# Means of the last six tiles by two DMAs through a DRAM row instead of TensorE transpositions

## What is computed

```python
xn = (x - mean(x)) / sqrt(var(x) + 1e-5)                # 2048 tokens x 512
q  = xn @ Wq.T + bq                                     # only every fourth head: 8 heads of 128
s  = elu(q) + 1
a  = s / (sum(s * z, per head) + 1e-6)
attn = repeat(a @ M, 4 heads) @ Wo.T                    # = a @ P, P = M @ (sum of Wo over the 4)
out  = x + attn + (xn @ (w * w_scale) + b)
```

## Time and profile before

| | us |
|---|---|
| median of 3 runs | 243.72 (243.65 to 243.77) |
| the profiled execution | 243.56 |
| its span, first to last instruction | 241.7 |
| PE busy | 234.1 (97%) |
| DVE busy | 178.0 (74%) |
| ACT busy | 119.6 (49%) |
| POOL busy | 108.4 (45%) |

### The profile page before, as it was taken

One profiled execution on the slowest core, in us unless ns is written; L12 is line 12 of the kernel. 1 busy time (PEld: TensorE's weight loads), 2 busy tenths in 40 slices (PEclk: granted clock), 3 DMA queues, 4 the chain that ended last, 5 costly groups with the idle time before them and its releaser, 6 DMA issues.

```text
span 241.7 us, 3385 instructions
## 1 busy us (share of the span) xinstructions
PE 234.1 (97%) x1030; PEld 186.7 (77%) x1030; DVE 178.0 (74%) x266; ACT 119.6 (49%) x276; POOL 108.4 (45%) x108
## 2 busy tenths in 40 slices
PE   8699999998999999999999999999999999999995
PEld 2488788885776788888888888888888888788885
DVE  2889695897998669887687694958666778995631
ACT  2654626628648923655463526455463747341110
POOL 1058734756271815553434326263403629657500
PEclk9999999999999999999999999999999999999999
DMA  7999999999370211424252515221212223244441
GB/s 225 405 417 411 383 242 225 216 217 217 94 252 5 53 51 52 127 54 126 53 168 53 161 50 169 52 91 42 88 52 73 56 75 108 76 136 136 133 174 44
DMA packets 21985, 34.83 MB, mean 144 GB/s; under 512 B 5200, under 2 KB 13136, under 8 KB 20816
## 3 DMA queue, kind: packets, MB, share of 16 engines
q1 hardware_dynamic: 19344, 26.63, 33.4%
q0 software_dynamic: 1376, 6.82, 13.4%
q10 hardware_dynamic: 1248, 1.18, 1.8%
HBM read 22.02 MB, written 4.19 MB: 108 GB/s over the span
## 4 chain that ended last, share of the span: by engine, by line
PE 33%; issue 31%; POOL 18%; DVE 8%; SPq 4%; DMA 2%; ACT 2%; ACTq 1%; POOLq 0%; DVEq 0%
POOL e_and_sz L313 9%; POOL xT L288 5%; PE attn_ps L793 4%; PE attn_ps L794 4%; PE attn_ps L795 4%; SPq L219 4%; POOL x L321 3%; PE q_ps L793 3%; PE q_ps L795 3%; PE q_ps L794 3%; DVE aT_lo L654 2%; PE dense_ps L793 2%; PE dense_ps L795 2%; PE dense_ps L794 2%; DMA xT<-in_xT 2%
## 5 line engine op out<-in xcount | busy, mean ns | idle before, releaser
L313 POOL TENSOR_TENSOR e_and_sz<-s,z_b 128x512 f32<-128x512 f32 x32 | 42.0, 1340 | 40.3 <-DVE den L633 40.2
L441 ACT ACTIVATE s<-s,rden 128x128 f32<-128x128 f32 x128 | 39.2, 389 | 40.5 <-DVE rden L637 40.5
L793 PE MATMUL attn_ps<-P_hi,aT_hi 128*128 128x512 f32 (+1 forms) x128 | 49.8, 389 | 0.5 <-DVE aT_lo L654 0.5
L795 PE MATMUL attn_ps<-P_hi,aT_lo 128*128 128x512 f32 (+1 forms) x128 | 49.1, 383 | 0.0
L794 PE MATMUL attn_ps<-P_lo,aT_hi 128*128 128x512 f32 (+1 forms) x128 | 49.0, 383 | 0.0
L793 PE MATMUL q_ps<-WqT_hi,xT_hi 128*128 128x512 f32 x104 | 42.1, 405 | 0.3 <-DVE s L628 0.3
L795 PE MATMUL q_ps<-WqT_hi,xT_lo 128*128 128x512 f32 x104 | 40.6, 390 | 0.0
L794 PE MATMUL q_ps<-WqT_lo,xT_hi 128*128 128x512 f32 x104 | 40.5, 389 | 0.0
L288 POOL TENSOR_TENSOR xT<-xT,mean_b 128x512 f32<-128x512 f32 x13 | 18.3, 1408 | 37.8 <-ACT mean_b L390 31.2
L621 DVE SCALAR_TENSOR_TENSOR q_ps<-q_ps,rstd,bq_b 128x512 f32<-128x512 f32 x28 | 21.0, 753 | 19.3 <-PE q_ps L795 19.3
L793 PEld LDWEIGHTS attn_ps<-P_hi,aT_hi 128*128 128x128 f32 x128 | 24.1, 188 | 6.2 <-issue 0.9
(11 more groups left out here) (82 smaller groups left out, 365.3 us busy)
## 6 DMA issues: line engine op xcount, KB each, us to landing
x<-in_WoT POOLq DMA_DIRECT2D x6, 1024.0 KB, 10.6
x<-in_x SPq DMA_DIRECT2D x16, 256.0 KB, 3.9
xT<-in_xT SPq DMA_DIRECT2D x16, 256.0 KB, 4.1
aT<-s SPq DMA_DIRECT2D x124, 32.0 KB, 1.9
out<-x SPq DMA_DIRECT2D x15, 256.0 KB, 2.3
MT<-s SPq DMA_DIRECT2D x96, 32.0 KB, 1.9
x<-in_WoT SPq DMA_DIRECT2D x2, 1024.0 KB, 14.0
s<-in_WqT SPq DMA_DIRECT2D x2, 512.0 KB, 7.1
```

The costliest lines, as they stand in the source:

```text
L313: nc.gpsimd.tensor_tensor(sz_eps[:, :, h * D // 2:(h + 1) * D // 2].rearrange("p g (j c) -> p j g c", j=2), by_quarter(sbuf_s[:, t % SRING ...
L441: last = nc.scalar.activation(a_g, a_g, ACT.Copy, scale=rden[:, t % 2, g:g + 1])
L793: nc.tensor.matmul(out, x_hi, w_hi, start=start, stop=False)
L795: return nc.tensor.matmul(out, x_lo, w_hi, start=False, stop=stop)
```

## The change

Tiles 0 to 9 keep their way. For tiles 10 to 15 (FIRST_BY_DMA is LEAD + 3 = 10), in steps 8 to 13:

- PE doesn't do `spread_mean(t + 2)`, and ACT doesn't do `copy_mean(t + 2)`.
- SP, after the loads of its step and ahead of `spread_blocks(t - 4)`, waits for bn_aggr of tile t + 2 and sends the column meanvar[:, t + 2, 0:1] (128 partitions, 4 bytes each) to row t + 2 of a new DRAM tensor, mean_rows: `line_up_mean`.
- ACT, at the place where copy_mean stood, waits until that row has landed (and for the buffer of mean_b, as copy_mean did) and issues a transfer that reads the row of 512 bytes into all 128 partitions of mean_b: `spread_mean_row`.
- POOL's `center` waits for the landing of that transfer instead of copy_mean.

```diff
--- before.py
+++ after.py
@@ -34,6 +34,7 @@
     XRING = 4
     HRING = 4
     BEHIND = 3
+    FIRST_BY_DMA = LEAD + 3
     assert P == D and HID == 512 and HALF == 512 and R == 4 and T == 16 and G == 8 and K == 4
 
     with ExitStack() as ctx:
@@ -65,6 +66,7 @@
         aT_hi = sb("aT_hi", [P, 2, G, P], F32R)
         aT_lo = sb("aT_lo", [P, 2, G, P], F32R)
         mean_b = sb("mean_b", [P, 2, P])
+        mean_rows = nc.dram_tensor("mean_rows", (T, P), F32)
         ident = sb("ident", [P, P])
         e_and_sz = sb("e_and_sz", [P, E + G * (D + 1)])
         neg_half = sb("neg_half", [P, 1])
@@ -116,6 +118,8 @@
         rstd_ready = sem("rstd_ready")
         mean_filled = sem("mean_filled")
         mean_copied = sem("mean_copied")
+        mean_row_in = [sem(f"mean_row_in{i}") for i in range(2)]
+        mean_b_in = [sem(f"mean_b_in{i}") for i in range(2)]
         xc_by_dve = sem("xc_by_dve")
         xc_by_pool = sem("xc_by_pool")
         xT_hi_ready = sem("xT_hi_ready")
@@ -219,6 +223,10 @@
                         sp.dma_start(aT_place(t)[j * 32:(j + 1) * 32, i, :],
                                      sbuf_s[i * 32:(i + 1) * 32, t % SRING, j * E // 4:(j + 1) * E // 4]
                                      ).then_inc(aT_in[in_MT(t)], 16)
+
+            def line_up_mean(t):
+                sp.wait_ge(meanvar_ready, t + 1)
+                sp.dma_start(mean_rows[t].unsqueeze(1), meanvar[:, t, 0:1]).then_inc(mean_row_in[t % 2], 16)
 
             def store(t):
                 sp.wait_ge(attn_added, t + 1)
@@ -261,6 +269,8 @@
                     sp.wait_ge(P_filled, t + 4 - FIRST_LENT + 1)
                     load_x(t + 4)
                     load_xT(t + 4)
+                if FIRST_BY_DMA <= t + 2 < T:
+                    line_up_mean(t + 2)
                 spread_blocks(t - BEHIND - 1)
                 if t - LEAD >= 1:
                     store(t - LEAD - 1)
@@ -283,7 +293,10 @@
                                         ).then_inc(rstd_ready, 1)
 
             def center(t):
-                pool.wait_ge(mean_copied, t - 2)
+                if t < FIRST_BY_DMA:
+                    pool.wait_ge(mean_copied, t - 2)
+                else:
+                    pool.wait_ge(mean_b_in[t % 2], 16 * ((t - FIRST_BY_DMA) // 2 + 1))
                 pool.wait_ge(xT_in[t], 16)
                 nc.gpsimd.tensor_tensor(xT[:, t % XRING, :, :], xT[:, t % XRING, :, :],
                                         mean_b[:, t % 2, :].unsqueeze(1).to_broadcast([P, K, P]), ALU.subtract
@@ -389,6 +402,11 @@
                     act.wait_ge(xc_by_pool, t - 4)
                 nc.scalar.activation(mean_b[:, t % 2, :], mean_ps[:, 0:P], ACT.Copy
                                      ).then_inc(mean_copied, 1)
+
+            def spread_mean_row(t):
+                act.wait_ge(mean_row_in[t % 2], 16 * ((t - FIRST_BY_DMA) // 2 + 1))
+                act.wait_ge(xc_by_pool, t - 4)
+                act.dma_start(mean_b[:, t % 2, :], mean_rows[t].unsqueeze(0).to_broadcast([P, P])).then_inc(mean_b_in[t % 2], 16)
 
             def copy_first_xT_hi(j):
                 act.wait_ge(xc_by_dve, j + 1)
@@ -526,8 +544,10 @@
                 if t == LEAD:
                     copy_P_hi(7)
                 copy_aT_hi(t - LEAD + 1)
-                if t + 2 < T:
+                if t + 2 < FIRST_BY_DMA:
                     copy_mean(t + 2)
+                elif t + 2 < T:
+                    spread_mean_row(t + 2)
                 for u in denominators_of_step(t):
                     if u < T - 2:
                         make_a(u)
```

## The result

The changed kernel takes 267.08 us (median of 6 runs, 265.94 to 268.94) against 243.69 us before: 1.0968 times as long (95% interval 1.0924 to 1.1012), 23.4 us slower where 1.3 were forecast. The profiled execution took 266.57 us, its span is 264.8.

A forecast was written before the change was run, and what follows sets the result against it. TensorE, busy 97% of the span, was taken as the bound; 0.66 us saved on transpositions and a 2.0 us stall at product_q(10, 0) gave +1.3 us on 243.72, so 245.0 us, range 243.9 to 246.7.

The forecast's parts named there:

- What bounds the kernel, and SyncE's backlog: Steps 8 to 13: TensorE's own work sets the pace; backlogged SyncE sends tile 10's row only at 110.24, mean ready at 96.38.
- the forecast's 119.3: Tile 10: predicted start of product_q(10, 0), wanted by TensorE at 117.31, so a stall of 2.0 us.
- 5.95: Tile 10: predicted us from the row's landing, through ScalarE's and VectorE's queued work, to TensorE's start of product_q(10, 0).
- I take 3.1 ... The bounds are 112.5 and 114.1: First transfer, tile 10: the row sent at 110.24 lands after 3.1 us, at 113.35, between those bounds.
- Rival (d): The two transfers in series bound tile 10: first 4.2 to 5 us, second 3; time 246.3 to 247.5; chance 12%.
- One stall, then, and not six: Tiles 10 to 15: TensorE stalls 2.0 us at product_q(10, 0) only; later tiles' rows come in time.
- The slack of 0.85 us at tile 11: product_q(11, 0): xT_lo(11) reaches TensorE at 132.05, wanted at 132.9, so the wait is hidden by 0.85 us.
- The second transfer: ScalarE's broadcast of the row into all partitions: lands 1.9 to 2.6 us after it is issued.
- It just hides behind make_a and exp.: Tile 10: the broadcast and centering let copy_xT_hi start by 3.4 to 4.2 us after landing; ScalarE's queue gets there at 4.24.
- The transpositions: TensorE, tiles 10 to 15: six removed at 0.11 us each save 0.66 us.
- SyncE's six added issues at 0: SyncE, steps 8 to 13: six issues of 0.53 us make 3.2 us, nearly all absorbed, so costed at 0.
- the spare 1.9 us: SyncE ahead of spread_blocks(10): about 1.9 us idle waiting for VectorE, expected to take up the added issues.

The follow-up runs named there:

- e8: The changed kernel with SyncE sending each tile's column of means one step sooner, still as adjacent 4-byte pieces: 244.12 us, ratio 1.0001.
- e2: The changed kernel with the first transfer as one 512-byte piece, a row of the identity, so wrong means are taken off: 245.03 us.
- e5: The kernel before, with one unused extra transfer of a different form on ScalarE's queue in each of steps 8 to 13: 243.88 us.
- e12: The changed kernel with the row's pieces 512 bytes apart in DRAM and the second transfer reading input b (wrong means), second run: 245.65 us.
- e10: The changed kernel with ScalarE's wait for the row and the second transfer moved behind make_a: 264.02 us.
- e4: The changed kernel without the first transfer; ScalarE issues the second at once from input b (wrong means): 242.58 us, ratio 0.9952.
- e1: The kernel before, plus the change's first transfer, for which nobody waits; means still go through TensorE: 243.59 us, ratio 0.9999.
- e7: The changed kernel with VectorE turning the means into four 128-byte pieces and ScalarE sending both transfers, the row behind exp_of(t, 0): 242.78 us, ratio 0.9955.
- e6: The changed kernel with both transfers on ScalarE, adjacent 4-byte pieces kept, its wait for the row behind make_a: 248.82 us, ratio 1.0185.
- e11: The changed kernel with VectorE turning the means so SyncE sends four 128-byte pieces at the change's own place: 247.16 us, ratio 1.0124.

## Why the prediction was wrong

**What bounds the kernel, and SyncE's backlog: right.** The row left at 111.57 (forecast 110.24; the load of x ahead of it took 1.28 us to issue in place of 0.58), ScalarE stood still from 101.4, GpSimd, copy_xT_hi, split_xT_lo and product_q(10, 0) followed in that order. e8 shows that the place is the other half of the cause: with the same slow row a step sooner there is no stall at any product_q. product_q(10, 0) started 8.0 us later than the forecast's 119.3: 5.3 by the landing, 1.3 by the row's later start and 1.4 by the way from the landing to TensorE (7.3 us in place of 5.95).

**The step that failed is the landing of the row, "I take 3.1 ... The bounds are 112.5 and 114.1".** It landed at 120.0, after 8.4 us. The bound from above, 3.8, was "the slowest of the transfers here", and all of those move pieces of 1 KB or more; I wrote that no row shows a write of 128 pieces and bounded it as if size didn't matter. Rival (d) had the right mechanism, the first transfer slow, and stopped at 5 us. e2 shows that no other term was off by much: with a landing of at most 2.3 us the time is 245.03, the forecast's 245.0. The sentence of the Trainium skill on writes to HBM ("DMA: Bandwidth & Descriptors", section on the anatomy of one DMA), weighed in (d), pointed the right way but not at the cause: e5 and e12 write the same pieces to the same memory in 2.6 and 2.8 us.

**"One stall, then, and not six" failed with it.** The slack of 0.85 us at tile 11 rested on a landing of 2.6 to 3.0. With 8 to 10 us the queues close a loop that the prediction left out, since it never asked what SyncE would come to wait for. The row of tile 10 holds ScalarE; so split_aT_lo(3) ends at 130.63; spread_blocks(5) waits for that and starts at 130.70; behind it, at 142.35, stands the row of tile 12, which lands at 150.4. The next rounds are the same: spread_blocks(7) at 161.17, (9) at 190.77, with tiles 11, 13, 15 in a second chain between. A round of two steps takes 30 us against TensorE's 27.2 (two of 13.60), which is the 1 to 3 us that nearly every tile is later than the one before it. This loop is read from the changed kernel's rows; e2, e8 and e12 agree with it, since with a short landing or an earlier place it doesn't form.

**The second transfer was under-sized:** 3.1 to 4.8 us for 1.9 to 2.6. The prediction says of its branch: "It just hides behind make_a and exp." With 4.1 us it is the longer one (e2: ScalarE waits 0.2 us for centering before copy_xT_hi; e10: moving make_a doesn't help). In e4 it is hidden.

**The transpositions:** 0.15 us each (e4), not 0.11, since the matmuls behind one start later as well. Six save 0.92 us; with that size the forecast's sum would have been lower by 0.3, so e2's 245.03 meets the forecast's 245.0 in part by luck: it saves 0.3 more and its stall is 2.2 us in place of 2.0.

**The clock: not priced at all.** After the idle time of 9.66 us the granted clock is at the lower of its two levels (1.2 GHz, 0.50):

```profile
127.30:131.70 4.40, 4.39 (x10) 3.47 (x11) 4.38 (x5) 1.03 (x2) 3.74 (x3) 0.50 0.00 0
...
203.50:208.00 4.50, 4.49 (x13) 3.57 (x14) 4.22 (x6) 1.22 (x3) 1.48 (x2) 0.62 0.06 15
...
227.30:231.60 4.30, 4.26 (x12) 3.39 (x13) 4.26 (x5) 0.00 (x0) 3.12 (x6) 0.60 0.41 125
```

product_q(10) took 7.7 us in place of 5.4. The clock is lower too at product_q(15) (7.2, behind an idle time of 2.25) and at product_attn(10) (behind 2.87), where nine matmuls have 3.7 us in place of 2.0. Together 5.7 us. TensorE's idle time from 98 to 252 us is 17.4 us against 0.5 before. 16.9 + 5.7 - 0.9 = 21.7 of the 23.0; the rest goes with the stalls, whose length by start times is longer than by the brackets (9.82 against 9.66 for the first), and wasn't split up further.

**SyncE's six added issues at 0:** right (e1), although they make spread_blocks(10) 3.15 us later and so more than the spare 1.9 us. e8 shows where it ends: another 1.5 us there costs TensorE 0.9 us more of waiting.

## What to carry to other kernels

A transfer's landing must be bounded by rows with its own piece size and its own spacing, or measured by itself first; one extra transfer per form in a kernel that ignores the result (e5) costs one run and would have shown this one's landing. A column of 4-byte values is best made contiguous on the chip (0.2 us of VectorE in e7) before it goes out. Before a wait is put on a queue that other waits depend on, follow what is queued behind it once around, until it comes back to the queue that sends; and price a stall of TensorE with the slow clock that may follow it.

## What the runs showed of the hardware

- 128 writes of 4 bytes side by side in DRAM land after 6.5 to 10.6 us, 32 of them after 3.0, the same 128 placed 512 bytes apart after 1.8 to 2.8, and to on-chip memory after 1.9. Why adjacent ones are slow wasn't tried further.
- While they are under way, other transfers' completions can be late: 8.8 us for a block transfer within the chip on another queue and 10.9 for a load (e6), where four pieces of 128 bytes in their place left 1.8 and 2.8 (e7); but only 4.1 to 4.3 for block transfers behind such a row in e5.
- An idle time of TensorE of 2.5 us was followed by a lower mean clock (0.61) in e11, which cost 1.7 us more, and by none in e12 (2.47 us). In the changed kernel those of 2.25 and 2.87 us were followed by mean clocks of 0.62 and 0.60, those of 0.18, 0.79 and 1.63 us by full clock. Those of 4.0 us (e6) and 9.7 us were followed by the lower level.
